# Two sets of PSUM banks and six store buffers for the last product of a two-layer attention and feed-forward kernel

## The reference: what is computed

```
grouped = x.reshape(b, s // g, g, d)                  # 128 groups of g = 32 tokens
logits = einsum('bntd,des->bntes', grouped, Wc) + bc + tie
perm = (logits == max over the 32 tokens)             # each of 32 x 4 experts takes one token of each group
permuted = einsum('bntd,bntes->bnesd', grouped, perm)
inner = relu(einsum('bnesd,esdf->bnesf', permuted, W1) + b1)      # 256 -> 32, first product
result_permuted = einsum('bnesf,esdf->bnesd', inner, W2) + b2     # 32 -> 256, second product
result = einsum('bnesd,bntes->bntd', result_permuted, perm)       # back to the tokens
```

## Time and profile before

| | us |
|---|---|
| median of 3 runs | 2045.28 |
| lowest and highest of the 3 | 2040.23 and 2054.05 |
| the profiled execution, its own time | 2038.18 |
| its span in the trace | 2036.4 |
| PE busy | 1793.9 (88%) |
| DVE busy | 1407.9 (69%) |
| ACT busy | 1141.8 (56%) |
| POOL busy | 777.6 (38%) |

### The profile page before, as it was taken

The page is one execution under the profiler, slowest core; times in us unless marked ns, Lnnn a source line. Parts: engine busy times, 40 slices in busy tenths (PEclk is TensorE's granted clock), DMA queues, the critical chain, the costliest instruction groups (busy, mean ns, idle before and its releaser), DMA issues.

```text
span 2036.4 us, 41318 instructions
## 1 busy us (share of the span) xinstructions
PE 1793.9 (88%) x15920; PEld 1487.0 (73%) x15920; DVE 1407.9 (69%) x2869; ACT 1141.8 (56%) x2830; POOL 777.6 (38%) x1160
## 2 busy tenths in 40 slices
PE   4789888886999899999999848999999999988546
PEld 3556666655999799999999747777777777866422
DVE  4677777753043198989898578999999998676221
ACT  1354545553443487777777447777677777744210
POOL 2112111111000133333333168788888887644000
PEclk8799999998999999999999969999999999998658
DMA  6434444312686566667677332122121221112689
GB/s 194 109 74 84 84 74 84 79 38 83 219 299 233 196 228 244 246 234 252 226 256 226 126 114 69 62 86 66 58 90 62 69 83 53 41 45 85 244 294 331
DMA packets 132054, 292.27 MB, mean 144 GB/s; under 512 B 13009, under 2 KB 77138, under 8 KB 116882
## 3 DMA queue, kind: packets, MB, share of 16 engines
q1 hardware_dynamic: 109458, 179.75, 28.8%
q0 software_dynamic: 18048, 105.69, 15.0%
q10 hardware_dynamic: 4352, 4.20, 0.6%
HBM read 203.60 MB, written 85.72 MB: 142 GB/s over the span
## 4 chain that ended last, share of the span: by engine, by line
PE 68%; DVE 13%; DMA 7%; issue 5%; POOL 3%; ACT 3%; SPq 0%; POOLq 0%; DVEq 0%
PE ps L1108 10%; PE ps L1122 9%; PE ps L1662 5%; PE ps L837 5%; PE ps L843 4%; PE ps L213 4%; PE ps L1693 4%; PE ps L1682 4%; PE ps L1648 4%; DMA R<-rp_scratch 3%; PE ps L351 2%; DVE NM L486 2%; DMA rp_scratch<-RP 2%; DVE NM L179 2%; PE ps L340 2%
## 5 line engine op out<-in xcount | busy, mean ns | idle before, releaser
L190 ACT ACTIVATE P<-ps,NM 128x256 f32<-128x256 f32 x512 | 235.6, 473 | 162.0 <-DVE NM L179 161.8
L203 POOL TENSOR_TENSOR P<-P,RS 128x1024 f32<-128x1024 f32 x128 | 245.2, 1916 | 93.9 <-DVE RS L197 93.5
L486 DVE TENSOR_REDUCE NM<-ps 128x2 f32<-128x512 f32 x256 | 164.7, 686 | 110.5 <-PE ps L328 110.4
L1108 PE MATMUL ps<-XRP,W1P 128*128 128x256 f32 x1872 | 228.1, 282 | 2.4 <-DVE W1P L1190 2.4
L1108 PEld LDWEIGHTS ps<-XRP,W1P 128*128 128x128 f32 x1872 | 221.3, 191 | 3.0 <-DVE W1P L1190 3.0
L1122 PE MATMUL ps<-W2P,HP 128*128 128x256 f32 x1872 | 221.7, 277 | 0.0
L596 ACT ACTIVATE PT<-ps 128x512 f32<-128x512 f32 x256 | 138.6, 593 | 142.8 <-PE ps L340 140.3
L1122 PEld LDWEIGHTS ps<-W2P,HP 128*128 128x128 f32 x1872 | 218.1, 188 | 0.0
L179 DVE TENSOR_REDUCE NM<-ps 128x2 f32<-128x512 f32 x256 | 164.3, 684 | 1.0 <-PE ps L1648 0.3
L137 POOL TENSOR_TENSOR LTMP<-RSTD 128x2 f32<-128x2 f32 (+1 forms) x156 | 33.2, 213 | 339.2 <-DVE RSTD L130 330.8
L1052 POOL DMA_INDIRECT WE<-in_we,WIX x39 | 44.2, 1133 | 305.6 <-DVE W1P L1190 200.8
(11 more groups left out here) (216 smaller groups left out, 3877.1 us busy)
## 6 DMA issues: line engine op xcount, KB each, us to landing
k_scratch<-KVS SPq DMA_DIRECT2D x64, 256.0 KB, 3.3
v_scratch<-KVS SPq DMA_DIRECT2D x64, 256.0 KB, 2.4
KS<-k_scratch SPq DMA_DIRECT2D x64, 256.0 KB, 3.1
V<-v_scratch SPq DMA_DIRECT2D x16, 1024.0 KB, 6.8
rp_scratch<-RP SPq DMA_DIRECT2D x16, 1024.0 KB, 5.9
R<-rp_scratch SPq DMA_DIRECT2D x16, 1024.0 KB, 14.0
QS<-q_scratch SPq DMA_DIRECT2D x96, 128.0 KB, 4.4
ys_scratch<-YS SPq DMA_DIRECT2D x39, 256.0 KB, 8.0
```

Source lines behind the costliest of these rows:

```text
L190: i = e.activation(self.P[u % 4][:, c, :], PS[SB[n % 3]][:, y * 256:y * 256 + 256], ACT.Exp, bias=self.NM[:, u % 4, c:c + 1], accum_out=se ...
L203: e.tensor_tensor(p, p, self.RS[:, u % 4, :].unsqueeze(2).to_broadcast([128, 4, 256]), ALU.mult).then_inc(self.s_pn, 1)
L486: e.tensor_reduce(NM0[b % 2][:, :, 8 * h + p], PS[SB[(2 * u + h) % 3]][:, :].rearrange("p (l j) -> p l j", l=2), AX.X, ALU.max, negate=Tru ...
L1108: m = e.matmul(PS[p][:, hh * 256:hh * 256 + 256], W1P[i % 2][wi][:, cc * 1024 + hc * 128:cc * 1024 + hc * 128 + 128], XRP[i % 2][xi][:, cc ...
```

## The change

It does four things in the last feed-forward, and nothing else in the program.

- DOWN becomes two sets of four banks. Steps 0 to 3 use the first set as before. From step 4 on the sets alternate, and the second is ps3, ps4, ps5, ps7, where the first product wrote. So from step 5 on `down(q2)` waits only for the banks of step q2 - 2 (`taken_of`), and step 4 and later wait for the last part of the first product to be through VectorE (`s_in` at 16).
- Four more store buffers, RP2 to RP5, in the place of PX. Steps 0 to 3 keep RP0 and RP1; steps 4 to 15 go through RP2 to RP5. `rp_free` asks for the store of step q2 - 2 at steps 2 and 3, for none at steps 4 to 7, and for that of step q2 - 4 from step 8 on. From step 4 on it also waits for the last `pe_up` (`s_u3` at 8).
- `pe_up(1, 2)` moves from behind step 3 to behind step 0, and `pe_up(1, 3)` from behind step 7 to behind step 1, with `dve_up` on VectorE.
- SP issues the loads `first(6)` and `first(7)` ahead of all stores.

```diff
+    RP += [mem_t(f"RP{i}", [128, 2, 4, 256], fp32) for i in range(2, 6)]
+    mem_t = Arena(nc, attn_at)
     R2 = [mem_t(f"R2{i}", [128, 8, 256], fp32) for i in range(NR)]
...
-    TURN, LOGIT, PERM, GATHER, DOWN = PS[0], PS[1], PS[2], (3, 4, 5, 7), (0, 1, 2, 6)
+    TURN, LOGIT, PERM, GATHER, DOWN = PS[0], PS[1], PS[2], (3, 4, 5, 7), ((0, 1, 2, 6), (3, 4, 5, 7))
...
+    def down_set(q2):
+        return q2 % 2 if q2 >= 4 else 0
+
+    def out_at(q2):
+        return q2 % 2 if q2 < 4 else 2 + q2 % 4
+
+    def out_of(q2):
+
+        return q2 - 2 if q2 in (2, 3) else q2 - 4 if q2 >= 8 else None
+
+    def taken_of(q2):
+
+        return q2 if q2 <= 4 else q2 - 1
...
-            w.wait_ge(s_e0, q2)
-            w.wait_ge(s_e1, q2)
+            w.wait_ge(s_e0, taken_of(q2))
+            w.wait_ge(s_e1, taken_of(q2))
+            w.wait_ge(s_in, 16 if q2 >= 4 else 0)
...
         for q2 in range(16):
             down(q2)
-            if q2 in (3, 7):
-                pe_up(e, w, 1, q2 // 4 + 2)
+            if q2 < 2:
+                pe_up(e, w, 1, q2 + 2)
...
     def rp_free(w, q2):
-        if q2 >= 2:
-            w.wait_ge(d_ks_rp[(q2 - 2) % 4], ks_sent + 16 * ((q2 - 2) // 4 + 1))
+        if q2 >= 4:
+            w.wait_ge(s_u3, 8)
+        p = out_of(q2)
+        if p is not None:
+            w.wait_ge(d_ks_rp[p % 4], ks_sent + 16 * (p // 4 + 1))
...
-                i = e.tensor_copy(RP[q2 % 2][:, :, r, :], PS[DOWN[r]][:, :].rearrange("p (q d) -> p q d", q=2))
+                i = e.tensor_copy(RP[out_at(q2)][:, :, r, :], PS[DOWN[down_set(q2)][r]][:, :].rearrange("p (q d) -> p q d", q=2))
...
         second(1)
+        first(6)
+        first(7)
         for q2 in range(16):
-            if q2 in (1, 5):
-                first(6 + q2 // 4)
             w.wait_ge(s_e0, q2 + 1)
```

More of the change, by code:

```diff
@@ L1352, in build @@
     s_fm, s_e0, s_e1, s_cm2, s_xo = sem("downmm3"), sem("rp0"), sem("rp1"), sem("returnmm"), sem("xout")
-    TURN, LOGIT, PERM, GATHER, DOWN = PS[0], PS[1], PS[2], (3, 4, 5, 7), (0, 1, 2, 6)
+    TURN, LOGIT, PERM, GATHER, DOWN = PS[0], PS[1], PS[2], (3, 4, 5, 7), ((0, 1, 2, 6), (3, 4, 5, 7))
     ks_sent = 32 * 16
-    UP_AT, GATHERED = 11, 19
+    UP_AT = 11
+    def down_set(q2):
[6 more added lines that the diff above has]
+        return q2 if q2 <= 4 else q2 - 1
     def pe_step(e, w, n):
@@ L1439, in down @@
                     rows = slice(32 * r, 32 * r + 32)
-                    m = e.matmul(PS[DOWN[r]][:, q % 2 * 256:q % 2 * 256 + 256], INT[rows, q, :],
+                    m = e.matmul(PS[DOWN[down_set(q2)][r]][:, q % 2 * 256:q % 2 * 256 + 256], INT[rows, q, :],
                                  WF2P[q // 8 % 2][rows, q % 8, :], start=True, stop=True)
@@ L1550, in dve_tail @@
             for r in range(2):
-                i = e.tensor_copy(RP[q2 % 2][:, :, r, :], PS[DOWN[r]][:, :].rearrange("p (q d) -> p q d", q=2))
+                i = e.tensor_copy(RP[out_at(q2)][:, :, r, :], PS[DOWN[down_set(q2)][r]][:, :].rearrange("p (q d) -> p q d", q=2))
             i.then_inc(s_e0, 1)
-            if q2 in (3, 7):
-                dve_up(e, w, 1, q2 // 4 + 2)
+            if q2 < 2:
+                dve_up(e, w, 1, q2 + 2)
         for b in range(16):
@@ L1579, in act_tail @@
             for r in range(2, 4):
-                i = e.activation(RP[q2 % 2][:, :, r, :], PS[DOWN[r]][:, :].rearrange("p (q d) -> p q d", q=2), ACT.Copy)
+                i = e.activation(RP[out_at(q2)][:, :, r, :], PS[DOWN[down_set(q2)][r]][:, :].rearrange("p (q d) -> p q d", q=2), ACT.Copy)
             i.then_inc(s_e1, 1)
@@ L1621, in sp_tail @@
         second(1)
+        first(6)
+        first(7)
         for q2 in range(16):
-            if q2 in (1, 5):
-                first(6 + q2 // 4)
             w.wait_ge(s_e0, q2 + 1)
             w.wait_ge(s_e1, q2 + 1)
-            e.dma_start(rpd[:, 8 * q2:8 * q2 + 8, :], RP[q2 % 2][:, :, :, :].rearrange("p q r d -> p (q r) d")).then_inc(d_ks_rp[q2 % 4], 16)
+            e.dma_start(rpd[:, 8 * q2:8 * q2 + 8, :], RP[out_at(q2)][:, :, :, :].rearrange("p q r d -> p (q r) d")).then_inc(d_ks_rp[q2 % 4], 16)
             if q2 in (3, 7):
```

## The result

The changed kernel takes 2032.06 us, the median of nine runs (2021.95 to 2042.63), against 2043.53 for the kernel before beside it (2039.37 to 2054.05). The ratio is 0.9944, with a 95% interval from 0.9923 to 0.9966: 7 to 16 us less, and less than 1%. In a second set of runs on another occasion the ratio was 0.9935 (0.991 to 0.996). The forecast was 8.6 us less, a time of 2036.7, and no change that a measurement could tell.

What follows compares the result with a forecast made beforehand. The store stage was held bound by alternating matmuls and copies, then by transfers after the change. Store 3 at 1920.3 plus 42.8 for 15 transfers gives 1963.1, 8.6 us earlier: 2036.7 us on the median, range 2024 to 2047.

Steps and rivals of the forecast that it cites:

- Transfers as the bound: Steps 4 to 15: engines deliver 1 MB each 2.13 us, faster than a 2.78 us transfer, so transfers bind.
- The price of a transfer: From store 3 on: 2.78 us per 1 MB at 377 GB/s, between 2.57 and 3.18; 15 transfers take 42.8 us.
- The start: Up to store 3: both loads and both quarters come first, so store 3 goes out at 1920.3, store 0 at 1903.4.
- The 2.3 us for stalls: In the two moved quarters: idle time charged at the earlier mean of 1.15 us each, bounds 0 and 3.65.
- Stalls as waits for instructions: In the late quarters: idle time without a releaser (3.65, 0.47, 0.47 us before) read as waits for instructions.
- The pace of steps: From step 5 on: matmuls run beside the previous step's copies, a step each 2.13 us in place of 3.47.
- The return: Behind the last landing: bound by transfers alone, untouched by the change, length kept at 64.7 us.
- The sum: Last store lands at 1963.1 against 1971.74, 8.6 us earlier; on the median 2036.7 us.
- The slower rival: Store queue: four stores under way hinder each other; at 290 GB/s the kernel is 3.1 us slower, 2048.4; chance 0.07.
- The rival of a late start: Moved quarters both stall 3.65 us or their weights land late: store 3 at 1925.3, 3.6 us won; chance 0.13.
- The larger gain: Higher clock gives three steps at 1.15, 2.9 us; with 408 GB/s and no stall 16.7 us won; chance 0.12.
- paid for by loads that no longer hold up stores 0 to 2: Ahead of store 3: the extra quarter's cost was taken as offset by the earlier loads, making this start no gain.

Runs made afterwards that it cites:

- half stores: The whole change with half of each store left out, the scratch's other half filled from weights early: stage 39.9 us, ratio 0.9951 to the kernel before.
- sets from step 8 on: The whole change with late quarters back behind steps 3 and 7, two bank sets and new buffers only from step 8: stage 56.4 us, ratio 0.9941.
- early weights: The whole change with both late quarters' weights fetched sooner, the first's into RP1's place, the second's into WF1P[0]: stage 56.3 us, ratio 0.9936.
- quarters behind steps 1 and 3: The whole change with the late quarters behind steps 1 and 3 instead of 0 and 1: stage 52.8 us, 2027.21 us, ratio 0.9906.
- the loads alone: The kernel before with only first(6) and first(7) issued ahead of all stores: stage 60.4 us against 68.3, ratio 0.9952.
- with the quarters moved: The kernel before with both loads and both late quarters moved, but one bank set and two store buffers: stage 64.4 us against 68.3, ratio 0.9967.
- the one profile with two loads moved away: The whole change with both second-product weight loads issued only after the first late quarter: 2034.37 us in one run, 73.0 us from gathers to last landing against 71.2.

## Why the prediction came out right, point by point

- **Transfers as the bound.** Right. From 1930 to the last landing the share is 0.95 at 385 GB/s, where 377 was forecast, and half stores take 15.8 us off.
- **The price of a transfer.** Forecast 2.78. From store 3's issue at 1930.6 to the last landing the 15 transfers took 41.8, against 42.8: 2.71 each behind the first. In the full stretch at 421 GB/s it is 2.49; part of the rest was lost from 1932 to 1936, at 297 GB/s and a share of 1.01. Why the rate was low there isn't shown. The copies of both engines beside it, 3.93 us of VectorE in 4, are not the reason: in the run with sets from step 8 on the rate was 418 GB/s from 1948.5 to 1953.5, with VectorE busy for 4.92 of 5 us. The rule that I weighed from the Trainium skill, "DMA: Bandwidth & Descriptors", section "Where 436 GB/s comes from" (about 358 GB/s for a core between the large memory and SBUF), does not hold here: 421 over 23 us.
- **The start.** Forecast: store 3 is 16.9 us after store 0 (1920.3 less 1903.4). Measured: 13.9. This is the term that was mis-sized, and most of the 4 us by which the stage beat the sum. Three things went differently in it. The loads took 6.2 and 8.5 us to land and not 5.2, the second beside the end of the first and then beside store 0, and PE waited 3.9 us for them. The 2.3 us for stalls did not show: neither moved quarter stalled in the two profiles of this kernel. With the weights there in time one did, by 2.61 us in the run with early weights, so that the wait for weights may have covered it. And steps 1 to 3 ran at 1.15, not at 2.13: the granted clock was 1.00 from 1916 to 1920 and from 1928 to 1932, which I had put into a rival. The errors offset each other in part.
- **Stalls as waits for instructions.** Supported, not shown. No row names the fetch, but the places of the stalls speak for it. Counted from the start of the tail on PE, the long stalls of all kernels, 1.33 to 3.65 us, stand behind matmul 110, 238, 365 or 493, that is 127 or 128 matmuls apart, or 256 instructions with their weight loads. The profile's queue q8, marked "instruction", moves a packet of 16 KB within about 1 us of the start of the long stalls that I looked at (those at 1906.0 in the changed kernel, 1910.5, 1915.0 and 1905.2 in three others). The Trainium skill, "Runtime: NRT & Kernel Launch", section "Instruction fetch mechanics", says that instructions are fetched in blocks of 16 KiB, which are 256 instructions, while the current block runs, and that the cost at a block's end is mostly hidden. The distance and the packet agree with that; hidden it isn't in these stalls. In others it is: PE passed matmul 366 in the changed kernel's first moved quarter, and 493 in the last one of the run with quarters behind steps 1 and 3, without a break, though the DMA share was 1.06 and 1.02. Transfers alone thus don't bring a stall about, and what decides is open.
- **The pace of steps.** Right on both sides: 3.50 with one set, and no such row with two. From step 8 on PE does wait for copies, 0.6 to 1.9, but behind copies that wait for stores.
- **The return.** Taken over as it was: 64.7 forecast, 64.4 measured.
- **The sum.** 8.6 us forecast, 12.6 in the stage, 11.5 between the medians, 7 to 16 by the interval. The slower rival falls: four stores in the queue give 421 GB/s, more than the 412 that was the best of several us before. The rival of a late start has half of its mechanism, PE's waits for late weights, but at 3.9 us and not 7.3, and store 3 was earlier than forecast and not later. The larger gain had the right cause, the clock, in part: three steps at 1.15 are the 2.9 us that it named. That the sum came within 4 us is partly luck, since too much for stalls and steps stood against too little for the loads.
- **What I did not see** is that the quarters' move is itself a loss. I wrote that it was "paid for by loads that no longer hold up stores 0 to 2"; taken apart, the loads alone give 7.9 and with the quarters moved 3.9. It earns its place only as what makes room for banks and buffers, and behind steps 1 and 3 it costs less.

## What to carry to other kernels

Where a stage shows both turns between two engines and waits for a buffer, take both away: either alone left the other standing, at 60 us in place of 56. Ask of every load behind a store whether it can go ahead of it into idle time; that was the largest single part, it was two lines, and the whole times don't show that the rest of the change brings more. And when transfers become the bound, what is left is how soon the queue fills: put first what produces the first stores, not what the later ones need.

## What the runs showed of the hardware

- With up to four 1 MB stores of 8 KB for each partition in the queue, and at times a load of weights, the engines moved 421 GB/s at a share of 1.00 over 23 us, and 297 at 1.01 in the 4 us from 1932, just before. Share alone does not tell the rate.
- In the run with the loads alone TensorE's granted clock was 1.00 for the 6.3 us behind a quarter of 128 matmuls and weight loads, and three steps took 1.15 us each; in the same run it was 0.50, and a step took 2.09, where each step had a wait behind it and no quarter between.
- PE's long stalls without a releaser, 1.3 to 3.7 us, stand 127 or 128 matmuls apart, 256 instructions with the weight loads, whatever the kernel. Transfers ran beside each of them, and in the one profile with two loads moved away none was left; but the same places were also passed without a stall at a DMA share above 1.
